# Attention kernel: lane 1's rows normalised before their transpose, its value products for two tiles at a time

## The reference

```python
# layer 0, for each image
h = group_norm(x, gn_w, gn_b).reshape(B, C, N)          # 32 groups, N = 1024
q, k, v = split(einsum('oc,bcn->bon', qkv_w, h) + qkv_b)
attn = softmax(einsum('bcn,bcm->bnm', q, k) * C**-0.5)  # 1024 x 1024
x = x + einsum('oc,bcn->bon', proj_w, einsum('bcm,bnm->bcn', v, attn)) + proj_b
# layer 1, for each image; q and k have 16 channels
attn = softmax(einsum('bdi,bdj->bij', q, k))
x = gamma * einsum('bcj,bij->bci', v, attn) + x
```

## Time and profile before

| What | Value |
| --- | --- |
| Median of 3 runs | 1571.02 us (1569.89 to 1573.38) |
| Profiled execution | 1575.76 us, its span 1573.7 us |
| Mean granted TensorE clock | 0.989 |
| PE matmul busy (modelled) | 1482.2 us, 94% of the span |
| DVE busy | 1285.6 us, 82% |
| ACT busy | 1218.2 us, 77% |
| GpSimd (POOL) busy | 1240.4 us, 79% |
| Chain that ended last | 66% on the SP queue at L299, 17% on PE |

### The profile page before, as it was taken

One profiled execution on the slowest core, in us unless ns is written; L12 is line 12 of the kernel. 1 busy time (PEld: TensorE's weight loads), 2 busy tenths in 40 slices (PEclk: granted clock), 3 DMA queues, 4 the chain that ended last, 5 costly groups with the idle time before them and its releaser, 6 DMA issues.

```text
span 1573.7 us, 43918 instructions
## 1 busy us (share of the span) xinstructions
PE 1482.2 (94%) x16777; PEld 1116.9 (71%) x16777; DVE 1285.6 (82%) x2508; ACT 1218.2 (77%) x1698; POOL 1240.4 (79%) x1027
## 2 busy tenths in 40 slices
PE   4899999999999999999899999999999999999977
PEld 2577777776777777777677777677777777777766
DVE  5678888888888888888788888888888878888885
ACT  3578878887877887878788887887878878888774
POOL 3788888888878887878788888788788878888653
PEclk9899999999999999999999999999999999999999
DMA  3799999999999999999999999999999999999999
GB/s 76 135 161 199 203 197 204 198 206 204 198 195 194 207 203 203 202 193 209 189 202 211 202 194 202 196 202 203 195 199 210 203 190 204 203 193 199 192 200 181
DMA packets 1081437, 305.21 MB, mean 194 GB/s; under 512 B 1068272, under 2 KB 1068944, under 8 KB 1081232
## 3 DMA queue, kind: packets, MB, share of 16 engines
q1 hardware_dynamic: 1066688, 270.42, 105.4%
q10 hardware_dynamic: 14544, 31.99, 6.0%
HBM read 17.13 MB, written 16.78 MB: 22 GB/s over the span
## 4 chain that ended last, share of the span: by engine, by line
SPq 66%; PE 17%; issue 5%; DVE 4%; DMA 3%; ACT 2%; POOL 1%; DVEq 0%; POOLq 0%; ACTq 0%
SPq L299 66%; DMA pt<-rows 3%; PE mixed L823 3%; PE mixed L825 3%; PE mixed L824 3%; PE scores L778 2%; DVE nmax L572 2%; PE scores L779 1%; PE scores L780 1%; DVE rows L589 1%; PE scores L808 1%; PE bank_w L889 1%; PE bank_w L897 1%; ACT scores L457 1%; POOL rows L358 1%
## 5 line engine op out<-in xcount | busy, mean ns | idle before, releaser
L823 PE MATMUL mixed<-v_head,pt 128*128 128x129 f16 x4096 | 719.5, 222 | 35.7 <-DMA pt<-rows 34.6
L572 DVE TENSOR_REDUCE nmax<-scores 128x1 f32<-128x1024 f32 x512 | 620.5, 1217 | 154.8 <-PE scores L808 141.8
L825 PE MATMUL mixed<-v_head,pt 128*128 128x129 f16 x4096 | 718.7, 220 | 0.0
L824 PE MATMUL mixed<-v_tail,pt 128*128 128x128 f16 x4096 | 718.7, 219 | 0.0
L358 POOL TENSOR_TENSOR rows<-prob,rows 128x1024 f16<-128x1024 f32 x256 | 545.4, 2130 | 21.3
L353 POOL TENSOR_SCALAR rows<-prob 128x1024 f16<-128x1024 f32 x256 | 267.9, 1046 | 233.4 <-ACT prob L452 229.9
L457 ACT ACTIVATE scores<-scores,nmax 128x1024 f32<-128x1024 f32 x256 | 278.7, 1089 | 204.2 <-DVE nmax L572 204.2
L823 PEld LDWEIGHTS mixed<-v_head,pt 128*128 128x128 f16 x4096 | 399.0, 97 | 47.1 <-DMA pt<-rows 45.6
L824 PEld LDWEIGHTS mixed<-v_tail,pt 128*128 128x128 f16 x4096 | 405.7, 99 | 2.3
L825 PEld LDWEIGHTS mixed<-v_head,pt 128*128 128x128 f16 x4096 | 397.0, 97 | 0.0
L589 DVE SCALAR_TENSOR_TENSOR rows<-scores,rows 128x1024 f16<-128x1024 f32 x256 | 313.0, 1222 | 35.6 <-ACT rows L465 35.4
(11 more groups left out here) (110 smaller groups left out, 1852.8 us busy)
## 6 DMA issues: line engine op xcount, KB each, us to landing
out_dram<-y ACTq DMA_DIRECT2D x64, 256.0 KB, 3.8
x_raw<-in_x_dram ACTq DMA_DIRECT2D x29, 512.0 KB, 5.2
pt<-rows SPq DMA_TRANSPOSE x512, 5.4
x_raw<-in_x_dram SPq DMA_DIRECT2D x3, 512.0 KB, 4.4
w_qkv<-in_L_conv_qkv_w_dram SPq DMA_DIRECT2D x3, 64.0 KB, 4.1
b_qk<-in_L_conv_bk_dram SPq DMA_DIRECT2D x8, 0.1 KB, 2.3
b_qk<-in_L_conv_bq_dram SPq DMA_DIRECT2D x8, 0.1 KB, 1.9
w_proj<-in_L_conv_proj_w_dram SPq DMA_DIRECT2D x1, 64.0 KB, 4.8
```

Of the source, the lines that this page charges most:

```text
L572: nc.vector.reduce_max(nmax[l][:, tile.i % TILES:tile.i % TILES + 1], scores[l][:, :], AX.X, negate=True).then_inc(maxed[l], 1)
L823: mm(mixed[l][:, 0:C + 1], head, vh[:, p, m, 0:C + 1], start=(m == 0), stop=False)
L824: mm(mixed[l][:, 0:C], head, vt[:, p, m, :], start=False, stop=False)
L825: done = mm(mixed[l][:, 0:C + 1], tail, vh[:, p, m, 0:C + 1], start=False, stop=(m == TILES - 1))
```

## The change

**Lane 1.** `exponent1` also gives the sum of its row (`accum_out=row_sum`). A new ACT instruction `sum_down` divides that sum by 4096, a new DVE instruction `invert1` takes its reciprocal, and `head_row1` and `tail_row1` scale by this reciprocal in place of the constant 4096. So the rows are already normalised when they are split, and lane 1's `norm`, its `back` and its old reciprocal fall away. `head_row1` now waits for `invert1`.

**Value products of lane 1.** Two tiles are taken together. The values are the stationary side and the two tiles' transposed rows the moving one (256 columns), so that the result stands channels by positions and needs no turn. A pair takes 24 matmuls, 12 in each of two slots (one half of the keys each), and one addition of 128 x 256 (`add_pair`) replaces two of 128 x 128. Lane 1's ring grows from 4 to 6.

**Order.** On DVE `invert1` stands behind lane 0's maximum, and the projections' tails stay between the two maxima. `add_pair` stands behind `tail_row1`.

**Image 2** and loads. Its statistics move from slot -1 to -3, its group-norm steps from slots 0 and 1 to -2 and -1, ahead of the scores; its load is issued ahead of sixteen small ones.

The diff, cut to its core:

```diff
-RING = 4
+RING = (4, 6)
+KEY_HALVES = (ATTEND, ATTEND + 1)
-STATS = Steps(-12, -11, first={1: (-11, -11), 2: (-9, -9)})
-GN = Steps(-10, -9, first={2: (-8, -7)})
-GN_BEHIND = 2
+STATS = Steps(-12, -11, first={1: (-11, -11), 2: (-11, -11)})
+GN = Steps(-10, -9)
...
+            load_first(2)
             for h in range(2):
                 for r in range(8):
...
-            load_first(2)
...
             def exponent1(tile):
+                at = slice(tile.i % TILES, tile.i % TILES + 1)
                 act.wait_ge(maxed[1], tile.i + 1)
-                nc.scalar.activation(scores[1][:, :], scores[1][:, :], ACT.Exp,
-                                     bias=nmax[1][:, tile.i % TILES:tile.i % TILES + 1],
-                                     scale=1.0).then_inc(exped[1], 1)
+                nc.scalar.activation(scores[1][:, :], scores[1][:, :], ACT.Exp, bias=nmax[1][:, at], scale=1.0,
+                                     accum_out=row_sum[:, at]).then_inc(exped[1], 1)
+                act.wait_ge(exped[1], tile.i + 1)
+                nc.scalar.activation(sum_down[:, at], row_sum[:, at], ACT.Copy,
+                                     scale=1.0 / P_UP).then_inc(summed_down, 1)
 
             def head_row1(tile):
...
-                act.wait_ge(exped[1], tile.i + 1)
+                act.wait_ge(inverted[1], tile.i + 1)
                 nc.scalar.activation(rows[1][:, tile.i % ROWS, 0, :], scores[1][:, :], ACT.Copy,
-                                     scale=P_UP).then_inc(row_headed[1], 1)
+                                     scale=rinv[1][:, tile.i % TILES:tile.i % TILES + 1]).then_inc(row_headed[1], 1)
...
+            def invert1(tile):
+                at = slice(tile.i % TILES, tile.i % TILES + 1)
+                dve.wait_ge(summed_down, tile.i + 1)
+                nc.vector.reciprocal(rinv[1][:, at], sum_down[:, at]).then_inc(inverted[1], 1)
...
+            def add_pair(pair):
...
+                dve.wait_ge(attended[1], pair[1].i // 2 + 1)
+                nc.vector.scalar_tensor_tensor(out=of_pair(into, pair),
+                                               in0=mixed[1][:, 0:2 * C].rearrange("p (t c) -> p t c", c=C),
+                                               scalar=1.0 / P_UP, in1=of_pair(residual[:, tile.p, :], pair),
+                                               op0=ALU.mult, op1=ALU.add).then_inc(done, 2)
...
                     row_max(tile)
                     exp_bias(tile)
-                added = [lane[slot - ADD] for lane in TILE_AT if slot - ADD in lane]
...
+                if tile := TILE_AT[1].get(slot):
+                    invert1(tile)
+                for tile in single_adds(slot):
+                    add_turned(tile)
                 if tile := TILE_AT[1].get(slot):
                     tail_row1(tile)
-                for lane in TILE_AT:
-                    if tile := lane.get(slot - ATTEND):
-                        invert(tile)
+                if tile := TILE_AT[0].get(slot - ATTEND):
+                    invert0(tile)
+                for pair in pair_adds(slot):
+                    add_pair(pair)
...
+            def attend_pair(pair, half):
...
+                into = mixed[1][:, 0:2 * C].rearrange("p (t n) -> p t n", n=C)
+                for m in range(half * PER_HALF, (half + 1) * PER_HALF):
+                    done = split_product(into, vh[:, p, m, 0:C], vt[:, p, m, :], pt[1][:, r:r + 2, m, :],
+                                         pt[1][:, r:r + 2, TILES + m, :], start=(m == 0), stop=(m == TILES - 1))
```

More of the change, by code:

```diff
@@ L31 @@
 PARTS = (K_SIDE, K_SIDE, Q_SIDE, Q_SIDE)
-TURNED = (slice(0, C), slice(C, 2 * C))
 X_BUFS = 3
@@ L271, in swings, with of_pair @@
         def swings(tile):
-            return 16 * (tile.i // RING + 1)
+            return 16 * (tile.i // RING[tile.lane] + 1)
+        def of_pair(image, pair):
+            first, step = pair[0].t, pair[1].t - pair[0].t
+            tiles = image.rearrange("p (t c) -> p t c", c=C)
+            first %= tiles.shape[1]
+            return tiles[:, first:first + step + 1:step, :]
         def qk_bank(im, j):
@@ L530, in body @@
                     qk1_copy(im, h)
-                for lane in range(2):
-                    if tile := TILE_AT[lane].get(slot - ATTEND):
-                        norm(tile)
+                if tile := TILE_AT[0].get(slot - ATTEND):
+                    norm(tile)
                 for im, part in W.at(slot):
@@ L936, in body @@
             def body(slot):
-                here = [lane.get(slot - ATTEND) for lane in TILE_AT]
-                for tile in here:
-                    if tile:
-                        attend(tile)
+                here = TILE_AT[0].get(slot - ATTEND)
+                if here:
+                    attend0(here)
+                for half, offset in enumerate(KEY_HALVES):
+                    if pair := pair_at(slot - offset):
+                        attend_pair(pair, half)
                 for im, part in W.at(slot):
```

148 lines of the change are left out of this document (85 added, 63 removed).

## The result

The changed kernel takes 1695.39 us (median of 4, 1693.16 to 1697.08) against 1570.64 us before: a ratio of 1.079, 95% interval 1.077 to 1.081. It is slower, as forecast, by 125 us and not by the forecast's 79: the forecast was 1650 us with a range up to 1688. The profiled execution took 1696.69 us, its span 1694.7.

The account below looks back on a forecast made before the run. PE, the transposes' queue and a four-engine loop lay close; the lengthened loop would bind. Its 48.3 us an image plus extras gave 49.95 against 47.28, +77 us steady, +76 in all: 1650 us, range 1618 to 1688.

Parts of the forecast that it names:

- The loop's own pieces: Lane 1's maximum to its next, through DVE and ACT: 6.12 us with a projection's tail, 5.78 without.
- from a reciprocal's start to ACT's next instruction 0.19 us: Step of lane 1's loop from DVE's reciprocal to ACT's head row: 0.19 us.
- head row to tail row 1.06 us, as now: Step of lane 1's loop from ACT's head row to DVE's tail row: unchanged at 1.06 us.
- the 0.37 us between 2.70 and 3.07 cover that: On ACT, an exponential 0.1 to 0.3 us late in slots with most copies stays hidden before the reciprocal.
- The third slot: Slot set by PE, without a projection's tail: 6.13 us instead of 5.78, +0.35 us an image.
- the statistics and `add_pair` terms: DVE work behind the tail row: +0.36 us for one slot's statistics, +0.42 us where statistics share with `add_pair`.
- a bound of -10 to 0: Start of the kernel: image 2's earlier group-norm steps save between 0 and 10 us, taken as -4.
- with hardly a projection's tail in them: The last 15 slots would take 5.8 us each, 87 us against 83.0: +4 us.
- The queue stays the bound: Rival: transposes still set the slots, reciprocal does not delay the head row; 1567 us, perhaps 1550; 8 in 100.
- PE drops to its low clock: Rival: PE idles about 1.2 us a slot, one slot per image runs slow; +130 us, about 1780; 4 in 100.
- The accumulator is dear: Rival: ACT's exponential takes a microsecond more for its accumulator output, every slot grows; 1800 us and above; 3 in 100.
- all extras at their upper ends: Upper case for the steady images: every addition to lane 1's loop at its largest, 51.5 us an image, about 1697 us.

Follow-up runs that it names:

- free_head: The changed kernel with the head row waiting only for the exponential and lane 1's rows scaled by the constant 4096, so not normalised: 1552.81 us, 0.988.
- norm_only: The kernel before with only lane 1's normalisation (row sum, sum_down, reciprocal) added, old attends, turns and image 2's slots kept: 1691.01 us, 1.076.
- wait_order: The changed kernel with the head row's two waits swapped, the one for the reciprocal first: 1679.86 us, 1.069.
- mem_scale: free_head with head row and tail row reading the scale 4096 from a 128 x 1 column in memory: 1554.89 us, 0.989.
- copy_ahead: The changed kernel with ACT's `qk1` copy moved ahead of lane 0's exponential: 1681.73 us, 1.071.
- before_img2: The kernel before with only image 2's new slots and its earlier load: 1566.2 us, 0.996.
- two_sums: The changed kernel with one more 128 x 1 ACT instruction in front of sum_down: 1715.94 us, 1.092.

## Why the prediction was wrong in size and right in kind

**The mechanism held.** The head row waits for the reciprocal 256 times, PE's largest wait is the tail row, PE no longer waits for DMA, the queue idles, and both waits on image 2's products are gone. The loop's own pieces were read right: 1.74 and 1.33 us became 1.73 and 1.32, and the reciprocal starts 3.05 us after the maximum, where 3.1 was foretold. The head row's wait is 0.53 us a slot instead of 0.8, and with 134.6 us it is not ACT's largest, as was foretold: the exponential's wait for the maximum is (174.4 us). `free_head` takes the loop away and all of the loss goes; `norm_only` puts in the loop alone and 118 of the 125 us come.

**Where the missing 45 us are.** Of the forecast's own parts:

| part | forecast | measured | difference in us |
|---|---|---|---|
| 29 steady images | 49.95 each | 51.00 each | +30.4 |
| up to the 9th maximum | 91.7 | 99.1 | +7.4 |
| last 15 slots | 87 | 93.4 | +6.4 |
| behind the last maximum | 22.8 | 23.3 | +0.5 |

**The steady images: terms mis-sized, one term missing.**

- *The last steps of the loop.* The step "from a reciprocal's start to ACT's next instruction 0.19 us" took 0.25: it was read from an instruction with its late wait alone, and here that wait is the second of two (`wait_order`: 0.06 us). The step "head row to tail row 1.06 us, as now" took 1.15: I gave the memory scale a price for the tail row and forgot it for the head row, which reads it too (`mem_scale`: 0.09 us). `tail_row1`'s own term, 0.03, was inside its bounds; `mem_scale` shows 0.06, of which the loop's last piece (1.81 for 1.80) shows 0.01. That makes 6.26 us where the sum had 6.15 (6.12 + 0.03): about +0.1 in each of six slots, and measured +0.07 to +0.16 in five of them. These two terms are the larger part of the miss in the steady images; `wait_order` alone, which takes back the first, brings 15.5 us.
- *A whole step missing*: the `qk1` copy on ACT, once an image, +0.43 us. I had followed what is queued behind the waiting head row as far as `norm` and the exponential of the next slot ("the 0.37 us between 2.70 and 3.07 cover that"), not to the copy, whose reader is PE. It is 29 x 0.43 = 12 us of the 30. `copy_ahead` shows it.
- *The third slot*, set by PE, is 6.02 us and not 6.13. The pairs do save time on PE there, for which I counted no gain. The first and the last of a pair's twelve matmuls on the changed kernel's PE, and what follows them:

```profile
765.24 0.27 PE L832 MATMUL mixed<-pt,v_head 128*128 128x256 f16 x1
...
766.44 0.27 PE L834 MATMUL mixed<-pt,v_tail 128*128 128x256 f16 x1
766.55 0.22 PE L832 MATMUL bank_w<-w_head,h_head 128*128 128x128 f16 x1
```

  Twelve take 766.55 - 765.24 = 1.31 us, where the working had 24 x 0.057 = 1.37: 0.06 us of the 0.11. The rest was not measured apart; in `norm_only`, with the old attends and both turns, this slot is as long as before (6.24).
- *What held*: the statistics and `add_pair` terms, whose two slots came out 6.71 and 6.65 us for 6.57 and 6.51, which is the loop's 0.1 again, and the third such term, 2.0 us from the tail row to the next maximum in the sixth slot, which came out 2.03.

The accumulator shows in the trace as an instruction of its own, ACTIVATION_READ_ACCUMULATOR, 0.19 us, just under my upper bound of 0.20. `sum_down` took the 0.20 us that the row gave. The 0.3 us that the prediction cites from the Trainium skill is given there for an ACTIVATE whose bias is one value per partition, and `sum_down` has no such operand. DVE waits for the sum only in slots without a projection's tail:

```profile
DVE rinv L626 <- ACT sum_down L497: 6.7, 32, 0.8
```

32 waits, one an image, 0.21 us each, where I had taken 0.1 an image; in the other such slot PE sets the time. The Trainium skill, VectorE: DVE Perf Modes, Two Vector instructions with no wait between them, says of the Vector engine that an instruction which also writes out its accumulator is two. The ACT rows of the changed kernel show the same of ScalarE.

**The start.** I let the steady sum begin at the 9th slot and gave the first eight only image 2's gain. The gain was there, and larger than taken: -6.8 us (`before_img2`). But the loop runs in those slots as well: from `free_head` to the changed kernel the 9th maximum moves from 89.2 to 99.1 us, 9.9 us, more than the gain. `norm_only`, without image 2's gain, has it at 100.0, and there the old wait still stands:

```profile
44.70 0.16 DVE L650 TENSOR_SCALAR gs<-bank_t 128x1 f32<-128x1 f32 x1 [5.61 <-PE bank_t L926]
```

The prediction said that "the loop is longer here too" and then put it inside a bound of -10 to 0, though it speaks for a positive end. Not all of the 7.4 us need be the loop's, for single executions differ here: `copy_ahead` reaches the 9th maximum at 99.3 us, `wait_order` at 97.0, and `two_sums`, whose chain is longer, at 95.7. In the changed kernel's execution the clock is 0.50 from 91.7 to 95.1 us, and its eighth slot takes 14.9 us, against 13.2 in `wait_order`, where the clock there is 1.00.

**The end.** The step "with hardly a projection's tail in them" was wrong. Ten of the last 15 slots have one, in the kernel before as well. 93.4 / 15 = 6.23 us a slot, against 6.38 in the steady part. The five slots without one take 6.00 us, not 5.8. The low clock (0.93 in the mean) may add to this; how much is not shown.

**The rivals.** *The queue stays the bound* fell: it idles 378 us. What it said of the queue held, though. With the loop out of the way (`free_head`) the queue does bind, at 1552.8 us, where the rival said 1567, or 1550 with PE's saved turns. *PE drops to its low clock* fell for the steady part, but not by much. PE waits 130 times for the tail row, 148.9 / 130 = 1.15 us each and in the steady images 1.74 us at most, and the clock stays at 1.00 (2.4 GHz) from 200 to 1500 us. Outside of it the clock did fall to 0.50: at 91.7 us, after PE had waited 2.21 us up to 90.41, at 1644.8 and 1665.2 us, after waits of 1.76 and 1.88 us, and at 1627.7 us, after this one:

```profile
1627.07 0.61 PE L862 MATMUL scores<-qk 64*128 64x512 f16 x4 [2.57 <-DVE rows L630]
```

The Trainium skill, TensorE: Matmul & The Clock Gate, has an idle array brought back to half rate; the trace agrees in these places. In `two_sums` waits of 1.84 us were followed by it in four images. There it cost 1.5 us each time, where the rival had 4.5. *The accumulator is dear* fell: its instruction takes 0.19 us, half of the 0.37 us of cover.

**The range.** Its upper end was taken with "the extras are each read from rows and not likely all absent", that is with an eye to its lower end. Every miss but the third slot went the same way, since nearly every one was a piece of chain that I had read at its value in a kernel in which it did not bind. The 1697 us of "all extras at their upper ends" stood in the working, and the result is 1695. That the two agree is chance: `add_pair`, the statistics and the accumulator came out near their middle, and what was missing were the 0.25 and 1.15 us, the copy, the start and the end. Nor does the working show how its 51.5 us an image come about; the two terms that it bounds, 0.4 and 0.8 us, give 50.8.

## What to carry to other kernels

Once a change closes a loop through several engines, its length is the time: read every piece of it with the operands and the waits that it will have, not as it stands now, where a neighbour may hide it. Then go through everything that is queued behind the instruction that waits, to the last reader, on each engine; here a copy of 0.63 us, for which PE had waited once in the whole kernel before (2.0 us), became 12 us. A number that DVE must give back to ACT in mid-slot costs its place in DVE's order: moving other work from ahead of it into the hole behind it brought 54 us, but only not needing it (`free_head`) brought all of the loss back.

## What the runs showed of the hardware

- A scale read from memory (one value per partition) instead of a constant: +0.089 us for ACT's copy of 128 x 1024 from PSUM (1007 to 1096 ns) and +0.058 us for DVE's two-input instruction of that size (1225 to 1283 ns).
- An accumulator output on ACT adds an ACTIVATION_READ_ACCUMULATOR of 0.194 us in the mean of 256, behind the exponential, whose own 1.09 us stay.
- Of two semaphore waits ahead of one ACT instruction, the order matters: with the one that is fulfilled last in first place, the instruction starts 0.06 us sooner after it. Over 256 instructions on a binding chain that was 15.5 us, 0.9% of the kernel.
- The same transpose held SP's queue for 1.99 us in the median in the changed kernel, whose queue has pauses, and for 2.72 us in the kernel before, whose queue is full. Inside the changed kernel those that follow directly on another take no longer than those after a pause (2.01 and 1.94 us).
- PE kept its 2.4 GHz through 1300 us in which it was busy 87%, with a wait of 1.74 us once an image. With 1.84 us at the same place (`two_sums`) the granted clock was 0.50 behind it for 3.4 us in 4 of 28 images, and each time the slot was 1.5 us longer.
